# A convolution and gated low-rank experts in split float32: first two tiles multiplied whole, low parts of the weights made later, kernel block spread from SBUF, table arguments on ScalarE

## The chip, the cores and the metric

One program runs on one core of a Trainium2 chip. The metric is the device time of one execution in microseconds; lower is better. The engines are TensorE (PE, its weight loads are PEld), VectorE (DVE), ScalarE (ACT), GpSimd (POOL) and SyncE (SP), which issues most of the DMAs. Each takes its instructions in the order in which they are written, and they wait for each other by semaphores.

## What is computed

```python
H, L = 64, 1024                      # heads, length; the batch is 64
dtA = (-exp(log_A_real) + 1j * A_imag) * exp(log_dt)[:, None]
K = 2 * einsum('hn,hnl->hl', Cs, exp(dtA[:, :, None] * arange(L))).real
y = causal_convolution(u * mask, K) + u * mask * D      # by FFT here
y = y * mask
scores = y @ Wr.T                                        # 64 experts
gates = softmax(top_k(scores, 16)), 0 elsewhere
h = einsum('nd,krd->nkr', y, A)                          # rank 16 each
out = x + 2.0 * einsum('nkr,kdr->nd', h * gates, B)
```

`x` is (64, 64, 1024) in float32, so 4096 rows of 1024 pass through the product with `A` (1024 x 1024), the router (1024 x 64) and the product with `B` (1024 x 1024).

## The kernel before, in words

The work is cut into 32 tiles (`TILES`) of two heads (`HT`) by 64 batches, which is 128 rows each. Every matrix product is made of three products in the format float32r: each operand is split into a high part (`*_hi`, a copy made by ScalarE) and a low part (`*_lo`, the subtraction `arrived - hi` made by VectorE), and hi x hi, hi x lo and lo x hi are summed in PSUM. The weights `a` and `b` are loaded once and stay in SBUF, in 17 pieces (`loads`: the router, eight of `A`, eight of `B`).

For a tile there are five kinds of work.

- **Tables.** `arguments(t)` on VectorE computes `args = grid * turns + phases`, for two heads and two phases of 130 elements, and takes the whole turns off. `waves(t)` on ScalarE makes `turned` (a sine) and `decay` (two exponentials); each of the two functions needs another table in ScalarE, so there is an `ACT_TABLE_LOAD` ahead of each. `make_powers(t)` multiplies the two, and `out_factors(t)` gives `out_raw`.
- **Convolution.** It runs in chunks of 128 positions. `turn_in` and `feed` on TensorE give what each chunk adds to a state, `first_states` and `states` on VectorE carry the state through seven chunks, `kernel_row` gives 128 values of `K`. ScalarE copies them to `k_sb` (`copy_k`), `add_skip` adds `D`, and two DMAs (`kernel_rows`, then `load_near`) take them to a padded row in HBM and back as a 128 x 128 block `t_lo`, in which each row stands one to the side of the row above. `near` multiplies with that block, `from_states` with the states.
- **Up.** `mask_y` masks the result, and `product_high` and `product_low` multiply it with `A` and the router in three column ranges (`H_PARTS`, 320 + 384 + 384 columns).
- **Gates.** `scores` go through two rounds of `max` and `match_replace` and two exponentials to `gates`; `hg` is the product of `h` and the gates, in three instructions, one per range.
- **Down.** `turn_hg` transposes `hg` in two halves, ScalarE copies them to `g_hi`, and 48 products of 512 columns with `B` give `out_ps`; `x_in` gets the rows of `x` plus the scaled result and is written out.

The work is staggered by hand. While `step(t)` multiplies tile t, it makes the states of tile t+1, the convolution's factors of tile t+2 and the tables of tile t+3. The order within each engine is that of the code. On TensorE a step is: the up products, `turn_hg` of half of `hg`, `near(t+1)`, `turn_hg` of the rest, `from_states(t+1)`, `turn_in(t+2)`, three quarters of the down products, `kernel_row(t+2)`, the rest of them, `feed(t+2)`. On VectorE, step t+1 follows directly on these rows of step t:

```python
dve.scalar_tensor_tensor(out=x_in[:, columns], ...)   # half 0
add_skip(t + 2)
make_powers(t + 3)       # waits for decay from ScalarE
dve.scalar_tensor_tensor(out=x_in[:, columns], ...)   # half 1
first_states(t + 2); states(t + 2, range(1, MIDDLE))  # now step t+1
# scores, top 16
states(t + 2, range(MIDDLE, FED))
# gates, hg in three parts
```

Ahead of step 0 stands a long start: the constants of the tables, and the low parts of all 17 pieces of the weights. `FIRST_B` products need the pieces of `A`, the down products those of `B`.

## Time and profile before

| | us |
|---|---|
| median of three runs | 970.09 (969.84 to 970.32) |
| the profiled execution's own time | 970.01 |
| its span, first to last instruction | 968.2 |
| PE busy | 909.8 (94%) |
| DVE busy | 734.9 (76%) |
| ACT busy | 350.6 (36%) |

The median is the time of the whole execution, and the span is what the profile's clock covers; 1.8 us lie around the span. The mean granted clock of TensorE over the span is 0.988 of full speed. A busy share is an average over a start, a long repeated part and an end, which have different limits.

### The profile page before, as it was taken

The numbers are of one execution on the slowest core, as the hardware profiler recorded it, in microseconds if no ns is written. First come the engines' busy times: TensorE is split into PE (matmuls) and PEld (weight loads), VectorE is DVE, ScalarE is ACT, GpSimd is POOL, SyncE is SP. The second block draws the span as 40 slices with busy tenths as digits, with TensorE's granted clock in tenths as the row PEclk, the third lists the DMA queues.
The fourth block names the chain that finished last, engine by engine and source line by source line (L and its number), as shares of the span: only waits on it lengthen the run. The fifth ranks groups of instructions, "written<-read, shape, count | busy, mean of one in ns | idle before, by whom it ended". The sixth has DMA issues, their size and how long they took to land.

```text
span 968.2 us, 15861 instructions
## 1 busy us (share of the span) xinstructions
PE 909.8 (94%) x4800; PEld 821.6 (85%) x4800; DVE 734.9 (76%) x2520; ACT 350.6 (36%) x569; POOL 1.3 (0%) x10
## 2 busy tenths in 40 slices
PE   0376999999999999999999999999999999999998
PEld 0265999988899998889999888999998899999887
DVE  7887877777788777778877777887777788777642
ACT  5543342334424333342333334333333433423210
POOL 0000000000000000000000000000000000000000
PEclk9977999999999999999999999999999999999999
DMA  7310212211221222112122211222221122222101
GB/s 272 145 50 22 67 54 70 70 52 51 59 70 49 70 70 62 49 54 67 49 70 70 70 49 49 65 53 66 70 70 49 49 65 64 55 70 71 48 25 44
DMA packets 27676, 63.63 MB, mean 66 GB/s; under 512 B 4816, under 2 KB 13200, under 8 KB 27664
## 3 DMA queue, kind: packets, MB, share of 16 engines
q1 hardware_dynamic: 27664, 63.49, 22.6%
q8 instruction: 6, 0.10, 0.0%
q14 instruction: 6, 0.05, 0.0%
HBM read 46.63 MB, written 16.84 MB: 66 GB/s over the span
## 4 chain that ended last, share of the span: by engine, by line
PE 91%; DVE 6%; ACT 1%; issue 1%; SPq 0%; DMA 0%; DVEq 0%; ACTq 0%
PE out_ps L751 24%; PE h_ps L751 18%; PE out_ps L755 12%; PE h_ps L755 9%; PE turn_ps L751 8%; PE turn_ps L755 4%; PE turn_ps L760 3%; PE conv_ps L736 2%; PE conv_ps L735 2%; PE conv_ps L734 2%; PE conv_ps L745 1%; PE conv_ps L746 1%; PE conv_ps L744 1%; PE conv_ps L727 1%; PE conv_ps L726 1%; PE conv_ps L725 1%
## 5 line engine op out<-in xcount | busy, mean ns | idle before, releaser
L751 PE MATMUL out_ps<-b_hi,g_hi 128*128 128x512 f32 x512 | 203.6, 398 | 0.0
L751 PE MATMUL out_ps<-b_lo,g_hi 128*128 128x512 f32 x512 | 200.5, 392 | 0.0
L751 PE MATMUL h_ps<-a_hi,y_hi 128*128 128x384 f32 x512 | 172.1, 336 | 0.0
L751 PE MATMUL h_ps<-a_lo,y_hi 128*128 128x384 f32 x512 | 172.0, 336 | 0.0
L755 PE MATMUL out_ps<-b_hi,g_lo 128*128 128x512 f32 x512 | 129.3, 395 | 0.0
L755 PEld LDWEIGHTS out_ps<-b_hi,g_lo 128*128 128x128 f32 x512 | 96.1, 188 | 22.4
L751 PEld LDWEIGHTS out_ps<-b_hi,g_hi 128*128 128x128 f32 x512 | 96.3, 188 | 19.3
L751 PEld LDWEIGHTS out_ps<-b_lo,g_hi 128*128 128x128 f32 x512 | 96.2, 188 | 19.2
L425 DVE TENSOR_TENSOR powers<-turned,decay 128x520 f32<-128x520 f32 x32 | 22.4, 700 | 110.6 <-ACT decay L283 110.5
L482 DVE SCALAR_TENSOR_TENSOR z<-swapped,step_other,part 128x64 f32<-128x64 f32 x384 | 92.4, 282 | 11.0
L755 PE MATMUL h_ps<-a_hi,y_lo 128*128 128x384 f32 x512 | 99.2, 336 | 0.0
L475 DVE SCALAR_TENSOR_TENSOR part<-z,step_own,conv_ps 128x64 f32<-128x64 f32 x384 | 90.5, 277 | 8.9
L751 PEld LDWEIGHTS h_ps<-a_hi,y_hi 128*128 128x128 f32 x512 | 96.1, 188 | 0.0
L751 PEld LDWEIGHTS h_ps<-a_lo,y_hi 128*128 128x128 f32 x512 | 96.1, 188 | 0.0
L688 DVE SCALAR_TENSOR_TENSOR x_in<-out_ps,gate_scale,x_in 128x512 f32<-128x512 f32 x64 | 47.9, 748 | 60.7 <-PE out_ps L755 60.7
L755 PEld LDWEIGHTS h_ps<-a_hi,y_lo 128*128 128x128 f32 x512 | 89.7, 188 | 0.0
L359 ACT ACTIVATE exp_all<-score_sb,neg_max 128x64 f32<-128x64 f32 x32 | 11.1, 348 | 206.7 <-DVE neg_max L634 206.7
L751 PE MATMUL turn_ps<-a_hi,y_hi 128*128 128x320 f32 x256 | 77.1, 314 | 2.0 <-DVE a_lo L503 2.0
L751 PE MATMUL turn_ps<-a_lo,y_hi 128*128 128x320 f32 x256 | 77.0, 314 | 0.0
L367 ACT ACTIVATE g_hi<-turn_ps 128x512 fp32r<-128x512 f32 x64 | 38.4, 600 | 83.7 <-PE turn_ps L760 83.7
L299 ACT ACTIVATE k_sb<-h_ps 1x256 f32<-1x256 f32 x32 | 12.0, 375 | 149.2 <-PE h_ps L716 149.0
L307 ACT ACTIVATE z_hi<-z 128x896 fp32r<-128x896 f32 x32 | 30.5, 954 | 95.0 <-DVE z L482 95.0
(159 smaller groups left out, 1479.8 us busy)
## 6 DMA issues: line engine op xcount, KB each, us to landing
xt_in<-in_xt SPq DMA_DIRECT2D x32, 512.0 KB, 3.3
x_in<-in_x SPq DMA_DIRECT2D x64, 256.0 KB, 3.6
out<-x_in SPq DMA_DIRECT2D x62, 256.0 KB, 3.1
a_in<-in_a_t SPq DMA_DIRECT2D x8, 512.0 KB, 8.9
b_in<-in_b_t SPq DMA_DIRECT2D x8, 512.0 KB, 14.4
t_lo<-k_padded SPq DMA_DIRECT2D x32, 128.0 KB, 2.9
k_padded<-k_sb SPq DMA_DIRECT2D x32, 1.0 KB
out<-x_in SPq DMA_DIRECT2D x4, 128.0 KB, 2.3
```

The lines of the kernel that those rows point to most:

```text
L307: act.activation(z_hi[:, :, :, :], z[:, :, :, :], ACT.Copy).then_inc(s_zhi, 1)
L367: act.activation(g_hi[:, 4 * bank:4 * bank + 4, :].rearrange("p c n -> p (c n)"), turn_ps[:, bank, :], ACT.Copy).then_inc(s_ghi, 1)
L425: dve.tensor_tensor(out=powers[:, :, :, :], in0=turned[:, :, :, :], in1=decay[:, :, :].unsqueeze(2).to_broadcast([P, HT, 2, W]), op=ALU.mu ...
L475: dve.scalar_tensor_tensor(out=part[:, i, :], in0=z[:, c - 1, i, :], scalar=step_own[:, bass.ds(n + i, 1)], in1=conv_ps[i][:, c * B:(c + 1 ...
L482: dve.scalar_tensor_tensor(out=z[:, c, i, :], in0=swapped[:, i, :], scalar=step_other[:, bass.ds(n + i, 1)], in1=part[:, i, :], op0=ALU.mu ...
L688: dve.scalar_tensor_tensor(out=x_in[:, columns], in0=out_ps[:, half, :], scalar=gate_scale[:, :], in1=x_in[:, columns], op0=ALU.mult, op1= ...
L734: pe.matmul(conv_ps[i][:, :], t_hi[:, i, :], xt_hi[:, i, :], start=True, stop=False)
L735: pe.matmul(conv_ps[i][:, :], t_hi[:, i, :], xt_lo[:, i, :], start=False, stop=False)
L736: last = pe.matmul(conv_ps[i][:, :], t_lo[:, i, :], xt_hi[:, i, :], start=False, stop=False)
L751: pe.matmul(o, hi[:, c, :], moving[:, c, columns], start=first and c == order[0] and moving is w_hi, stop=False)
L755: last = pe.matmul(o, lo[:, c, :], w_hi[:, c, columns], start=False, stop=c == order[-1])
L760: last = pe.transpose(turn_ps[:, c // 4, (c % 4) * P:(c % 4 + 1) * P], hg[:, c * P:(c + 1) * P], ident[:, :])
```

## The change

It has four parts.

1. **Whole float32 for tiles 0 and 1** (`EXACT = 2`). The products of these two tiles (feed, kernel row, near, from states, up) multiply float32 operands as they are (`whole_*`), and the splits of `out_raw`, `xt`, `z`, `y`, `in` and `t` are dropped for them. The down products keep the three float32r products. The first tile's convolution gets its output in `out_ps` in two halves (`conv_0`), so that the first half of `y` can be masked and multiplied early.
2. **Low parts later.** Four pieces of `B` (`EARLY`) get their low parts from TensorE and ScalarE: `whole_b` computes `arrived - hi` in PSUM with an identity and a negated identity, ScalarE copies it out. Four (`MIDST`) stay on VectorE ahead of step 0. The nine pieces of `A` and the router (`LATE`) are subtracted by VectorE in step 1. The remaining loads are issued behind `load_near(0)`.
3. **The block from SBUF.** `k_sb` is now itself padded, and `load_near` reads the shifted rows straight out of its one partition, in one DMA per head. The write to HBM is gone.
4. **Arguments on ScalarE.** From tile 1 on the four rows `grid * turns + phase` are four ScalarE instructions (`theta`), each with a scale and a bias that are read from a column. `waves(t)` becomes `sines(t)`, `theta(t + 1)`, `decays(t)`. Half of the parameter loads are issued by ScalarE.

The diff, cut to what matters:

```diff
+EXACT = 2
...
+        EARLY = [FIRST_B + c for c in (4, 5, 6, 7)]
+        MIDST = [FIRST_B + c for c in (3, 2, 1, 0)]
+        LATE = list(range(FIRST_B))
+        HIGH = EARLY + LATE[:3] + MIDST + LATE[3:]
+        REST_PS = [turn_ps, out_ps, turn_ps, out_ps]
...
             def load_near(t, first=False):
                 if not first:
                     sp.wait_ge(s_near, t)
-                    sp.sem_inc(s_freed, 1)
-                sp.wait_ge(s_k, 16 * t + 16)
-                src = bass.AP(k_dram, t * (HT * KROW), [[1, P], [KROW, HT], [1, P]])
-                sp.dma_start(t_lo[:, :, :].bitcast(F32), src).then_inc(s_t, 16)
+                sp.wait_ge(s_kdone, t + 1)
+                for i in range(HT):
+                    row = k_sb[:, i, :]
+                    shifted = bass.AP(row.tensor, row.offset, [[HT * KROW, 1], [1, P], [1, P]])
+                    sp.dma_start(t_lo[:, i, :].bitcast(F32), shifted).then_inc(s_t, 16)
...
-            def waves(t):
-                act.wait_ge(s_args, t + 1)
-                act.activation(turned[:, :, :, :], args[:, :, :, :], ACT.Sin, scale=TWO_PI).then_inc(s_wave, 1)
-                for i in range(HT):
-                    act.activation(decay[:, i, :], grid[:, 0, :], ACT.Exp, scale=rates[:, bass.ds(HT * t + i, 1)]).then_inc(s_wave, 1)
+            def theta(t):
+                act.wait_ge(s_sine, t)
+                for i in range(HT):
+                    turn = turns[:, bass.ds(HT * t + i, 1)]
+                    act.activation(args[:, i, 0, :], grid[:, :], ACT.Identity, scale=turn, bias=phase_own[:, :]).then_inc(s_theta, 1)
+                    act.activation(args[:, i, 1, :], grid[:, :], ACT.Identity, scale=turn, bias=phase_other[:, :]).then_inc(s_theta, 1)
...
                 if table:
-                    waves(t + 3)
+                    sines(t + 3)
+                    if not last_table:
+                        theta(t + 4)
+                    decays(t + 3)
             step(0, first=True)
-            with act.Fori(LOOP, END) as t:
+            step(1)
+            with act.Fori(LOOP, END - 1) as t:
                 step(t)
+            step(TILES - 4, last_table=True)
...
             def arguments(t):
-                for i in range(HT):
-                    dve.scalar_tensor_tensor(out=args[:, i], in0=grid[:, :, :], scalar=turns[:, bass.ds(HT * t + i, 1)],
-                                             in1=phases[:, :, :], op0=ALU.mult, op1=ALU.add).then_inc(s_theta, 1)
-                dve.wait_ge(s_theta, HT * t + HT)
+                dve.wait_ge(s_theta, 2 * HT * t + 2 * HT)
...
+            step(1, weights=LATE)
...
+            def whole_b(n):
+                _, arrived, hi, _ = loads[EARLY[n]]
...
+                for half in range(2):
+                    columns = slice(half * HALF, (half + 1) * HALF)
+                    pe.matmul(REST_PS[n][:, half, :], ident[:, :], arrived[:, columns], start=True, stop=False)
+                    last = pe.matmul(REST_PS[n][:, half, :], minus[:, :], hi[:, columns], start=False, stop=True)
...
+            def whole_product(n, c):
+                o, c0, width, _ = H_PARTS[n]
+                return pe.matmul(o, y_m[:, c, :], a_in[:, c, c0:c0 + width], start=c == 0, stop=c == NC - 1)
...
+            pe.wait_ge(s_minus, 3)
+            whole_b(0)
             turn_in(0)
-            feed(0, first=True)
-            kernel_row(0)
-            near(0)
-            from_states(0)
...
+            whole_b(1)
+            whole_feed(0)
+            whole_row(0, k_ps)
+            whole_b(2)
+            whole_b(3)
+            whole_near_0()
+            whole_from_states_0(0)
+            first_step()
+            step(1, whole=True)
+            pe.wait_ge(s_wlo, len(MIDST) + len(LATE))
```

Three places in the order of the instructions carry the prediction. The first is the end of ScalarE's repeated step, from the copy of the kernel row (`k_sb`) to the end of the loop. Before:

```order
L299 ACTIVATE k_sb<-h_ps 1x256
L280 REGISTER_ALU
L281 ACT_TABLE_LOAD
L281 ACTIVATE turned<-args 128x520
L283 ISA
L283 ACT_TABLE_LOAD
L283 ACTIVATE decay<-grid,rates 128x130
L283 ISA
L283 ACTIVATE decay<-grid,rates 128x130
```

The same place in the changed kernel:

```order
L335 ACTIVATE k_sb<-h_ps 1x2x128
L307 REGISTER_ALU
L308 ACT_TABLE_LOAD
L308 ACTIVATE turned<-args 128x520
L303 ISA
L303 ACTIVATE args<-grid,phase_own,turns 128x130
L304 ACTIVATE args<-grid,phase_other,turns 128x130
L303 ISA
L303 ACTIVATE args<-grid,phase_own,turns 128x130
L304 ACTIVATE args<-grid,phase_other,turns 128x130
L314 ISA
L314 ACT_TABLE_LOAD
```

Four instructions now stand between the sine and the table load that the two `decay` rows follow.

The second place is VectorE's step 1 of the changed kernel, from the low part of the gated `hg` (`g_lo`) to the add of the first half of `x_in`:

```order
L730 TENSOR_TENSOR g_lo<-turn_ps,g_hi 128x512 x2
L551 TENSOR_TENSOR y_m<-conv_ps,mask 128x8x64 x2
L497 TENSOR_TENSOR o_lo<-out_raw,o_hi 128x260
L501 TENSOR_TENSOR in_lo<-h_ps,in_hi 128x256
L571 TENSOR_TENSOR a_lo<-a_in,a_hi 128x8x64
L571 TENSOR_TENSOR a_lo<-a_in,a_hi 128x1024 x3
L565 TENSOR_TENSOR y_lo<-y_m,y_hi 128x8x64 x2
L515 TENSOR_TENSOR xt_lo<-xt_in,xt_hi 128x1024
L571 TENSOR_TENSOR a_lo<-a_in,a_hi 128x1024 x5
L470 TENSOR_SCALAR turned<-args 128x520
L472 TENSOR_TENSOR args<-args,turned 128x520
```

Nine subtractions for the weights stand there that stood ahead of step 0 before, and the two rows of `arguments` are behind them.

The third place is the start of TensorE, up to the first product with `A`. Before, the first rows were two transposes, the feed, the kernel row and the near products in threes:

```order
L709 MATMUL h_ps<-ident,powers 128x128 x2
L725 MATMUL conv_ps<-xt_hi,in_hi 128x448
L726 MATMUL conv_ps<-xt_lo,in_hi 128x448
L727 MATMUL conv_ps<-xt_hi,in_lo 128x448
L725 MATMUL conv_ps<-xt_hi,in_hi 128x448
```

In the changed kernel the subtractions for `b` stand around them:

```order
L845 MATMUL h_ps<-ident,powers 128x128 x2
L837 MATMUL out_ps<-b_in,ident 128x512
L838 MATMUL out_ps<-b_hi,minus 128x512
L837 MATMUL out_ps<-b_in,ident 128x512
L838 MATMUL out_ps<-b_hi,minus 128x512
L874 MATMUL conv_ps<-xt_in,in_whole 128x448 x2
L856 MATMUL h_ps<-out_raw,real 128x256
```

Each threefold product has become a single one on whole operands, and four products for a piece of `b` come ahead of the feed; two more pieces follow before the near products.

## Rows read from the trace of the kernel before

**Rows 1.** The page: the span.
```profile
span 968.2 us, 15861 instructions
```

**Rows 2.** Busy time by stretch: us, PE, PEld, DVE, ACT, POOL (instructions), PE clock, DMA.
```profile
50.00:60.00 10.00, 7.52 (x25) 6.79 (x26) 7.28 (x11) 3.28 (x6) 0.00 (x0) 0.50 0.37 106
70.00:80.00 10.00, 0.00 (x0) 0.00 (x0) 9.17 (x35) 1.72 (x4) 0.00 (x0) 0.71 0.00 0
491.00:519.00 28.00, 28.00 (x151) 25.37 (x150) 21.89 (x76) 10.23 (x18) 0.00 (x0) 1.00 0.22 61
```

**Rows 3.** Timeline of PE: start, duration, what, idle before; tiles 0, 0, 1, 16.
```profile
55.06 0.60 PE L751 MATMUL turn_ps<-a_hi,y_hi 128*128 128x320 f32 x1 [2.01 <-DVE a_lo L503]
...
80.36 1.11 PE L760 MATMUL turn_ps<-ident,hg 128*128 128x128 f32 x4 [10.77 <-DVE hg L658]
...
98.60 0.31 PE L751 MATMUL turn_ps<-a_hi,y_hi 128*128 128x320 f32 x1
...
519.90 0.31 PE L751 MATMUL turn_ps<-a_hi,y_hi 128*128 128x320 f32 x1
```

**Rows 4.** Busy groups of VectorE until 98.6 us: busy us, mean ns, idle before.
```profile
L503 DVE TENSOR_TENSOR b_lo<-b_in,b_hi 128x1024 fp32r<-128x1024 f32 x8 | 9.3, 1219 | 0.2 <-ACT b_hi L276 0.2
L503 DVE TENSOR_TENSOR a_lo<-a_in,a_hi 128x1024 fp32r<-128x1024 f32 x8 | 9.2, 1218 | 0.0
```

**Rows 5.** Waits between 300 and 600 us: total us, times, longest us.
```profile
DVE powers L425 <- ACT decay L283: 37.2, 10, 3.7
...
DVE x_in L688 <- PE out_ps L755: 14.3, 11, 1.3
```

**Rows 6.** Timeline from a kernel row on TensorE to the powers on VectorE.
```profile
514.86 0.28 PE L716 MATMUL h_ps<-o_lo,real 128*128 128x256 f32 x1
...
515.18 0.38 ACT L299 ACTIVATE k_sb<-h_ps 1x256 f32<-1x256 f32 x1 [4.91 <-PE h_ps L716]
...
517.52 1.28 ACT L283 ACT_TABLE_LOAD   x1
...
518.82 0.70 ACT L283 ACTIVATE decay<-grid,rates 128x130 f32<-128x130 f32 x2
519.55 0.70 DVE L425 TENSOR_TENSOR powers<-turned,decay 128x520 f32<-128x520 f32 x1 [3.72 <-ACT decay L283]
```

**Rows 7.** Timeline of `hg` on VectorE and the weight loads that need it.
```profile
502.65 0.55 DVE L658 TENSOR_TENSOR hg<-h_ps,gates 128x384 f32<-128x384 f32 x1
504.51 0.55 DVE L658 TENSOR_TENSOR hg<-h_ps,gates 128x384 f32<-128x384 f32 x1
...
503.49 0.53 PEld L760 LDWEIGHTS turn_ps<-ident,hg 128*128 128x128 f32 x4
...
505.26 0.59 PEld L760 LDWEIGHTS turn_ps<-ident,hg 128*128 128x128 f32 x4
```

**Rows 8.** Busy groups of ScalarE over the span.
```profile
L283 ACT ACTIVATE decay<-grid,rates 128x130 f32<-128x130 f32 x64 | 22.4, 397 | 0.4
...
L359 ACT ACTIVATE exp_all<-score_sb,neg_max 128x64 f32<-128x64 f32 x32 | 11.1, 348 | 206.7 <-DVE neg_max L634 206.7
...
L276 ACT ACTIVATE b_hi<-b_in 128x1024 fp32r<-128x1024 f32 x8 | 7.7, 1043 | 0.0
...
L333 ACT ACTIVATE far_decay<-rates 128x64 f32<-128x64 f32 x1 | 0.3, 256 | 0.0
```

**Rows 9.** Timeline: parameter loads on the SP queue, first powers on VectorE.
```profile
0.74 3.63 SPq L211 DMA_DIRECT2D par<-in_parameters  x8
...
18.39 0.70 DVE L425 TENSOR_TENSOR powers<-turned,decay 128x520 f32<-128x520 f32 x1
```

**Rows 10.** The chain that ended last, at full clock: start, us, what.
```profile
102.29 2.78 PE h_ps L751 x16
...
110.61 0.44 PE turn_ps L760 x4
```

**Rows 11.** DMA issues: count, KB each, median us from issue to landing.
```profile
t_lo<-k_padded SPq DMA_DIRECT2D x32, 128.0 KB, 2.9
```

More of the change, by code:

```diff
@@ L250, in step @@
                     fetch_rows(t + 1)
-            step(0)
+            for t in range(LOOP):
+                step(t)
             with sp.Fori(LOOP, END) as t:
@@ L368, in step @@
                                    ACT.Copy).then_inc(s_ghi, 1)
+                if first:
+                    for i in LATE[6:]:
+                        split_weights(i)
+                    sines(2)
+                    theta(3)
+                    decays(2)
                 if prep:
@@ L371, in step @@
                     high_in(t + 2)
-                if conv:
+                if conv and not first:
                     for i in range(HT):
@@ L396, in link, with mark, after @@
                 dve.wait_ge(s_calc, calc[0])
+            def mark(ins):
+                calc[0] += 1
+                ins.then_inc(s_calc, 1)
+                return calc[0]
+            def after(count):
+                dve.wait_ge(s_calc, count)
             def exp_parts(v):
@@ new lines, in _ @@
+            dve.tensor_tensor(out=u, in0=a, in1=a, op=ALU.mult)
+            squares = mark(dve.tensor_tensor(out=v, in0=aim, in1=aim, op=ALU.mult))
+            after(angle)
+            nearest = mark(dve.tensor_scalar(kk, im, INV_2PI, ROUND, ALU.mult, ALU.add))
+            after(squares)
+            square = mark(dve.tensor_tensor(out=den, in0=u, in1=v, op=ALU.add))
+            after(nearest)
+            nearest = mark(dve.tensor_scalar(kk, kk, ROUND, None, ALU.subtract))
+            dve.tensor_copy(skip[:, :], par[0:1, 5, :])
@@ new lines, in add_rows, with first_step @@
+            def add_rows(t, half):
+                columns = slice(half * HALF, (half + 1) * HALF)
+                dve.wait_ge(s_down, 2 * t + half + 1)
+                dve.scalar_tensor_tensor(out=x_in[:, columns], in0=out_ps[:, half, :], scalar=gate_scale[:, :],
+                                         in1=x_in[:, columns], op0=ALU.mult, op1=ALU.add).then_inc(s_o, 1)
+            def first_step():
+                gate(0)
+                gates_of(0)
+                gate_part(0, 0)
+                gate_part(0, 1)
+                sum_gates()
+                first_states(1)
+                add_skip(1)
+                states(1, range(1, 3))
+                gate_part(0, 2)
+                states(1, range(3, 5))
+                low_gated(0, 0)
+                low_gated(0, 1)
+                states(1, range(5, FED))
+                arguments(2)
+                make_powers(2)
+                out_factors(2)
+                for i in range(HT):
+                    mask_y(1, i)
+                low_in(2)
+                low_out(2)
+                low_x(2)
+                scale_of(0)
+                add_rows(0, 0)
+                arguments(3)
+                add_skip(2)
+                make_powers(3)
+                add_rows(0, 1)
@@ new lines, in step @@
+            def step(t, conv=True, prep=True, table=True, weights=()):
+                if conv:
+                    first_states(t + 1)
+                    states(t + 1, range(1, MIDDLE))
+                gate(t)
+                if conv:
+                    states(t + 1, range(MIDDLE, FED))
+                gates_of(t)
+                gate_part(t, 0)
+                gate_part(t, 1)
+                if conv:
+                    low_near(t + 1)
+                    low_z(t + 1)
+                sum_gates()
+                gate_part(t, 2)
@@ L673, in step @@
                     low_in(t + 2)
+                for i in weights[:4]:
+                    low_weights(i)
                 if conv:
@@ L773, in step, with turn_hg, down_high @@
                     if n == 0:
-                        pe.wait_ge(s_ylo, HT * t + HT)
+                        pe.wait_ge(s_ylo, HT * (t - EXACT) + HT)
                     product_low(o, y_lo, a_hi, slice(c0, c0 + width), range(NC)).then_inc(s_up, 1)
+            def turn_hg(blocks):
+                for c in blocks:
+                    last = pe.transpose(turn_ps[:, c // 4, (c % 4) * P:(c % 4 + 1) * P], hg[:, c * P:(c + 1) * P], ident[:, :])
+                return last
+            def down_high(half, order, first=False):
+                product_high(out_ps[:, half, :], g_hi, b_hi, b_lo, slice(half * HALF, (half + 1) * HALF), order, first)
@@ new lines, in step @@
+            def step(t, conv=True, prep=True, whole=False):
+                pe.wait_ge(s_glo, 2 * t)
+                if whole:
+                    pe.wait_ge(s_ym, HT * t + HT)
+                    pe.wait_ge(s_kcopy, t + 2)
+                    for n in range(len(H_PARTS)):
+                        for c in range(NC):
+                            last = whole_product(n, c)
+                        last.then_inc(s_up, 1)
+                else:
+                    pe.wait_ge(s_yhi, HT * (t - EXACT) + HT)
+                    up(t, conv)
```

527 lines of the change are left out of this document (302 added, 225 removed).

## The prediction

> **What bounds the kernel now.** I read the page first (the span [rows 1]), then the busy time by stretch. In a stretch of 28 us in the middle TensorE is busy for all of it and VectorE for 21.9 [rows 2]: the repeated part is bound by TensorE. A tile takes (519.90 - 98.60) / 15 = 28.09 us [rows 3]. The start is another matter: tile 1 begins only at 98.60, after a gap of 10.77 us in which TensorE waits for `hg`, because VectorE has 9.2 + 9.3 us of subtractions for the weights in its queue [rows 3, 4]. So the start can be shortened, and the rest can only get longer, by a wait of TensorE.
>
> The next question is how near such a wait is, since the change adds work to ScalarE in every tile. The waits of the middle say that VectorE stands idle 3.7 us per tile ahead of `powers`, for `decay` [rows 5]. Such an idle time looks like slack, and it is none. The timeline shows a loop. TensorE makes a kernel row at 514.86, ScalarE copies it at 515.18, and only then come the sine, the table load and `decay`; VectorE makes `powers` at 519.55 [rows 6]. Behind it stand the second half of `x_in`, the states of the next tile, the gates and `hg`. One period before, at 519.55 - 28.09 = 491.46, the same `powers` began, and the second part of `hg` ended at 502.65 + 0.55 = 503.20, 11.74 us later [rows 6, 7]. Of VectorE's idle time per tile (28.0 - 21.9 = 6.1 [rows 2]) 3.7 lie ahead of `powers` and 1.3 ahead of `x_in` [rows 5], so this stretch is nearly without a gap. TensorE loads that part of `hg` at 503.49; the third part ends at 504.51 + 0.55 = 505.06 and is loaded at 505.26 [rows 7]. With 0.04 us for the signal (`decay` ends at 519.52, `powers` begins at 519.55 [rows 6]) the slack is 0.25 and 0.16 us. Whatever makes `decay` later by more than 0.16 us makes TensorE wait in every tile.
>
> **The repeated part after the change.** `theta` puts four ScalarE rows between the sine and the table load ahead of `decay`. VectorE loses its two rows of `arguments` in return, but these are ahead of the wait for `down` (1.3 us idle [rows 5]) and gain nothing there. The price of a row: `decay` has 130 elements and one operand read from a column and takes 0.397; two of them take 0.70, so one overlaps the next by 0.10 [rows 6, 8]. `theta` has a second such operand, its bias. `exp_all` (64 elements, a bias column) takes 0.348 and `far_decay` (64, none) 0.256 [rows 8], so I add 0.09: 0.49 each. Four take 4 x 0.49 - 3 x 0.10 = 1.66, and 0.04 for the wait for the sine makes 1.70. The wait of TensorE is 1.70 - 0.16 = 1.54 us per tile. The lower bound is a second column that costs nothing: 4 x 0.397 - 0.3 + 0.04 = 1.33, a wait of 1.17. The upper is no overlap: 1.96 + 0.04, a wait of 1.84. I take the middle one, since each part of it has a row. Which tiles: a `theta` row in step t delays `hg` of tile t+1. It stands in the steps to 27, so tiles 3 to 28 wait, 26 of them (tiles 1 and 2 are counted in the start): 26 x 1.54 = 40.0 us, with 30.4 and 47.8 as bounds.
>
> **The start after the change**, by when each piece begins.
> - First powers: 18.39 before. Eight parameter loads take 3.63 us of issuing on one queue [rows 9]; split over two queues they take half, and land 1.4 us earlier after the first of the others. About 2 us of small operations move behind `powers`. I take 15.0.
> - Price of products: 16 of 384 columns take 2.78, so a column costs 0.45 ns at full clock [rows 10]. A whole float32 product holds all four products of two halves by two halves, and the split form three of them, so I count four times the float32r time. The nearest row is lower: four transposes of float32 operands take 0.44 for 4 x 128 columns, 0.86 ns, 1.9 times [rows 10]; that is my lower bound.
> - The Trainium skill says in FP8 and Floating Point Precision, under TensorE Precision Notes, that true FP32 needs four passes through the array. By that the sum stays; by the transposes' row it would be 3 us less. No row here shows such a product.
> - Clock: the stretch from 50 to 60 us runs at 0.50, the lower level of 1.2 GHz, after TensorE had mostly idled [rows 2]. I count the low level until about 23 us.
> - Transposes 15.8 to 16.5, the copy and a 1.04 us copy of a piece of `b` [rows 8] to 18.2; `whole_b(1)` is 2 x 512 x (4 + 1) columns, 4.6 at the low clock, to 22.8; the feed 896 x 4 columns, 3.2, to 26.0; the row and two more pieces of `b` 0.5 + 4.6 + waits to 31.4; a copy, near products and the first half of the states' 1.2 + 2.6 to 35.2; mask. First up product at 36.2, against 55.06 [rows 3]: it no longer waits for the low parts of `a`.
> - Up products of tile 0: 8 x 1088 columns x 4 x 0.45 ns = 15.8; a transpose, a feed, a row and a half of the states lie in between, 3.2; a last wait of 1.1 for `hg`. `turn_hg` at 56.3, against 80.36 [rows 3].
> - From there to tile 1 it took 98.60 - 80.36 = 18.2 and takes about the same (two fewer high-low triples, two whole products). Tile 1 begins at 74.4, 24.2 earlier.
> - Tile 1: its up products take 15.8 where 24 x 1088 columns took 11.8, + 4.0. The kernel row of tile 2 now follows the whole of the down products, and `theta` comes into the loop, a wait of 1.3. And VectorE has nine subtractions, 9.2 + 0.6 us [rows 4], in this step, all ahead of `arguments`; tile 2 waits for them, 1.6. Together + 6.9.
> - Tile 2: `arguments`, sine and `decay` stand behind these subtractions, so `powers` comes about 5.5 us after the tile's first product instead of 0.35 before it (519.55 against 519.90 [rows 3, 6]). Less the slack that is 5.7 us of waiting.
> - Tile 3 began at 98.60 + 2 x 28.09 = 154.8 and now begins 24.2 - 6.9 - 5.7 = 11.6 us earlier.
>
> The block from SBUF replaces two DMAs in a row by one. In the repeated part nobody waits for it: it is issued at about 516 [rows 6] and used after 503.49 + 28.09 = 531.6 [rows 7], with 2.9 us to landing [rows 11]. In the start I count the same 2.9. The Trainium skill says in SBUF — State Buffer, under Door 1: The DMA port swizzle, that a DMA's bandwidth goes by the number of 16 ports its partitions reach; one partition reaches one. An estimate from its 435 GB/s over 16 ports is 27 GB/s, 4.8 us for the 128 KB. It would delay the near products of tile 0 by some 2 us and end at 1000; no row here has a DMA out of one partition.
>
> **Sum.** 968.2 - 11.6 + 40.0 = 996.6 us of span, + 1.8 around it (970.01 - 968.2) = 998.4. The profiled execution is 0.08 below the median, which is nothing here. I say 998.
>
> **Rivals.**
> - *The delay is absorbed* (faster). If ScalarE runs the four rows in little time, or VectorE's stretch behind `powers` has slack that I don't see, the start's gain remains, and grows, since tiles 1 and 2 wait 1.3 and 1.6 us less: 11.6 + 2.9 = 14.5, so 955.5. It decides where 26 waits equal the gain: about 0.5 us per tile, that is four rows in 0.7. For it speaks that the idle time ahead of `powers` is long; against it every row above: two `decay` rows alone take 0.70 [rows 8, 6]. 8 in 100.
> - *The clock falls in each wait.* TensorE ran at the low level at 55.06, behind a gap of 2.0 us [rows 2, 3]. If 1.5 us of waiting brought 5 us at half speed in each tile, as from 55.06 to 60, it would cost 2.5 us more in each of 26: 1063. Against it: before 55 us it had been idle most of the time, and would be busy 95% here. 4 in 100.
> - *The start gains nothing*: the clock stays low to 40 us and beyond, or the late loads of `a` and `b` hold up the up products. Then 970.0 + 40.0 + about 4 = 1014. 6 in 100.
> - The forecast has 81 in 100, and 1 is left for a sum that ends within 0.2%.
>
> **Numbers.** The start gives 11.6, with 19 if the float32 products cost 1.9 times and the clock is full from the first, and 4 if it is low until 40 us and the block is late. The low end is 970.0 + 30.4 - 19 = 981, the high end 970.0 + 47.8 - 4 = 1014; I take 980 to 1014. A change of 0.2% (1.9 us) is about what a measurement of this kernel can tell from none. Faster: 8 in 100; the same: 1; slower: 91.
>
> **What would show it.** In the middle, TensorE waits about 1.5 us per tile ahead of `turn_hg`, released by `hg`, the period is 29.6 us, and `powers` waits 5.4 for `decay`. Four ScalarE rows of 0.49 stand between sine and table load. Tile 1 begins near 74, tile 2 near 109, tile 3 near 143, with a wait of 5 to 6 us in tile 2. Wrong would be a period of 28.1, `theta` rows under 0.2 us, or a tile 3 at 155.

## The result and the profile after

The changed kernel takes 998.75 us, the median of 4 runs (997.6 to 1001.69), the kernel before 970.02. The ratio is 1.0299, 95% interval [1.0287, 1.0311]: slower by 3%. The forecast was 998.0. The profiled execution of the changed kernel took 997.6 us, the fastest of the four; its span is the row below.

**The page of the changed kernel**: the span.

```profile
span 995.8 us, 15699 instructions
```

**Timeline of TensorE, changed kernel**: the first up product of tile 0, the first transpose of tile 0's `hg`, tile 1, tile 1's `hg`, tile 2, tile 2's `hg`, tile 3 and tile 16. These answer to [rows 3].

```profile
35.21 0.78 PE L937 MATMUL turn_ps<-a_in,y_m 128*128 128x320 f32 x2 [0.96 <-issue]
...
54.21 0.98 PE L950 MATMUL turn_ps<-ident,hg 128*128 128x128 f32 x7 [1.11 <-DVE hg L723]
...
72.27 4.47 PE L937 MATMUL turn_ps<-a_in,y_m 128*128 128x320 f32 x16
76.57 10.48 PE L937 MATMUL h_ps<-a_in,y_m 128*128 128x384 f32 x32
89.34 0.66 PE L950 MATMUL turn_ps<-ident,hg 128*128 128x128 f32 x4 [2.28 <-DVE hg L723]
...
107.49 0.41 PE L928 MATMUL turn_ps<-a_hi,y_hi 128*128 128x320 f32 x1 [1.72 <-DVE a_lo L571]
...
124.48 1.11 PE L950 MATMUL turn_ps<-ident,hg 128*128 128x128 f32 x4 [4.87 <-DVE hg L723]
...
142.89 0.31 PE L928 MATMUL turn_ps<-a_hi,y_hi 128*128 128x320 f32 x1
...
527.73 0.31 PE L928 MATMUL turn_ps<-a_hi,y_hi 128*128 128x320 f32 x1
```

The start is shorter by 154.8 - 142.89 = 11.9 us at tile 3. From there a tile takes (527.73 - 142.89) / 13 = 29.60 us, where it took 28.09. The waits of the middle say why (between 300 and 600 us: total us, times, longest us), beside [rows 5]:

```profile
DVE powers L479 <- ACT decay L314: 54.2, 10, 5.4
...
PEld turn_ps L950 <- DVE hg L723: 17.4, 20, 1.5
PE turn_ps L950 <- DVE hg L723: 11.9, 10, 1.2
```

VectorE now waits 5.4 us for `decay` instead of 3.7, and TensorE, which waited for nothing here, stops in every tile for `hg`: its weight loads 1.5 us, its transposes 1.2 us, since the loads had run ahead of the products. The loop itself, in the changed kernel's timelines of ScalarE, VectorE and the weight loads (against [rows 6, 7]):

```profile
495.22 0.64 ACT L308 ACTIVATE turned<-args 128x520 f32<-128x520 f32 x1
496.00 0.50 ACT L303 ACTIVATE args<-grid,phase_own,turns 128x130 f32<-128x130 f32 x1
496.40 0.48 ACT L304 ACTIVATE args<-grid,phase_other,turns 128x130 f32<-128x130 f32 x1
496.79 0.48 ACT L303 ACTIVATE args<-grid,phase_own,turns 128x130 f32<-128x130 f32 x1
497.18 0.48 ACT L304 ACTIVATE args<-grid,phase_other,turns 128x130 f32<-128x130 f32 x1
497.68 1.28 ACT L314 ACT_TABLE_LOAD   x1
498.97 0.70 ACT L314 ACTIVATE decay<-grid,rates 128x130 f32<-128x130 f32 x2
...
499.70 0.70 DVE L479 TENSOR_TENSOR powers<-turned,decay 128x520 f32<-128x520 f32 x1 [5.42 <-ACT decay L314]
...
510.88 0.55 DVE L723 TENSOR_TENSOR hg<-h_ps,gates 128x384 f32<-128x384 f32 x1
...
511.48 0.42 PEld L950 LDWEIGHTS turn_ps<-ident,hg 128*128 128x128 f32 x4 [1.51 <-DVE hg L723]
```

Read it as a chain: the sine ends at 495.86, the table load that `decay` needs starts at 497.68. The four rows between, with 0.14 us of waiting for the sine ahead of them, take 1.82 us. `powers` follows 0.03 us behind `decay`, the second part of `hg` ends 11.73 us after `powers` began (511.43; before it was 11.74), and its load follows at 511.48, 1.51 us late. Nothing on the way has absorbed the delay.

Busy time of the changed kernel by stretch (us; PE, PEld, DVE, ACT, POOL; PE clock; DMA), beside [rows 2]:

```profile
124.00:130.00 6.00, 5.52 (x19) 4.74 (x20) 4.16 (x11) 1.53 (x3) 0.00 (x0) 0.57 0.00 0
491.00:519.00 28.00, 26.82 (x145) 24.16 (x144) 19.42 (x73) 11.97 (x21) 0.00 (x0) 1.00 0.31 61
```

In the middle the clock stays at its full level, 2.4 GHz, in spite of a wait in every tile. Behind the 4.87 us wait of tile 2 it does not: 0.57 over 6 us.

### The profile page after: what moved, and what is told of

It reads as the page before. It is cut to its first block, busy times and chain, and to the rows that moved or that the text cites. A ratio compares the mean times of both kernels' runs of the same rounds, so it can differ in the third digit from the quotient of the medians.

```text
span 995.8 us, 15699 instructions
## 1 busy us (share of the span) xinstructions
PE 933.1 (94%) x4772; PEld 817.2 (82%) x4772; DVE 693.2 (70%) x2443; ACT 392.7 (39%) x685; POOL 2.0 (0%) x12
## 4 chain that ended last, share of the span: by engine, by line
PE 43%; DVE 28%; ACT 15%; issue 10%; DMA 1%; DVEq 1%; ACTq 1%; SPq 0%
PE out_ps L928 18%; DVE z L542 7%; PE out_ps L932 6%; DVE swapped L537 5%; DVE part L535 5%; ACT L314 4%; ACT L308 3%; PE turn_ps L950 3%; DVE x_in L743 2%; ACT decay L314 2%; DVE hg L723 2%; ACT turned L308 2%; ACT args L303 2%; PE h_ps L928 2%; ACT args L304 2%
## 5 line engine op out<-in xcount | busy, mean ns | idle before, releaser
L928 PE MATMUL h_ps<-a_hi,y_hi 128*128 128x384 f32 x480 | 163.3, 340 | 0.0
L928 PE MATMUL h_ps<-a_lo,y_hi 128*128 128x384 f32 x480 | 161.6, 337 | 0.0
L932 PEld LDWEIGHTS out_ps<-b_hi,g_lo 128*128 128x128 f32 x512 | 96.1, 188 | 21.2
L932 PE MATMUL h_ps<-a_hi,y_lo 128*128 128x384 f32 x480 | 94.5, 339 | 0.0
L928 PEld LDWEIGHTS h_ps<-a_lo,y_hi 128*128 128x128 f32 x480 | 90.2, 188 | 0.0
L928 PEld LDWEIGHTS h_ps<-a_hi,y_hi 128*128 128x128 f32 x480 | 90.0, 188 | 0.0
L932 PEld LDWEIGHTS h_ps<-a_hi,y_lo 128*128 128x128 f32 x480 | 85.3, 188 | 0.0
L950 PE MATMUL turn_ps<-ident,hg 128*128 128x128 f32 x256 | 41.1, 285 | 39.4 <-DVE hg L723 39.4
L950 PEld LDWEIGHTS turn_ps<-ident,hg 128*128 128x128 f32 x256 | 28.0, 143 | 56.4 <-DVE hg L723 55.7
L928 PE MATMUL turn_ps<-a_hi,y_hi 128*128 128x320 f32 x240 | 71.0, 309 | 1.7 <-DVE a_lo L571 1.7
L928 PE MATMUL turn_ps<-a_lo,y_hi 128*128 128x320 f32 x240 | 70.8, 309 | 0.0
```

The costliest lines, as they stand in the source:

```text
L928: pe.matmul(o, hi[:, c, :], moving[:, c, columns], start=first and c == order[0] and moving is w_hi, stop=False)
L932: last = pe.matmul(o, lo[:, c, :], w_hi[:, c, columns], start=False, stop=c == order[-1])
L950: last = pe.transpose(turn_ps[:, c // 4, (c % 4) * P:(c % 4 + 1) * P], hg[:, c * P:(c + 1) * P], ident[:, :])
```

## The experiments

The period of a kernel is read in its trace from two starts of the transposes of `powers` in the repeated part, 26 tiles apart. For the changed kernel:

```profile
130.21 0.38 PE L845 MATMUL h_ps<-ident,powers 128*128 128x128 f32 x2
...
899.96 0.38 PE L845 MATMUL h_ps<-ident,powers 128*128 128x128 f32 x2
```

(899.96 - 130.21) / 26 = 29.61 us. All kernels read in this way, with the median of the runs and the interval of the ratio to the kernel before:

| kernel | time, us | ratio to before | period, us |
|---|---|---|---|
| before | 970.0 | 1 | 28.09 |
| changed | 998.75 | 1.0287 to 1.0311 | 29.61 |
| decay_first | 956.24 | 0.9839 to 0.9871 | 28.16 |
| half_theta | 976.07 | 1.0046 to 1.008 | 28.83 |
| theta_alone | 1014.75 | 1.0438 to 1.0473 | 29.64 |
| args_vector | 964.17 | 0.992 to 0.9953 | 28.36 |
| spare_tile | 965.88 | 0.9941 to 0.9974 | 28.36 |
| rows_hbm | 959.71 | 0.9885 to 0.992 | 28.16 |
| args_early | 954.2 | 0.9818 to 0.9851 | 28.16 |
| decay_ahead | 955.6 | 0.9839 to 0.9871 | 28.16 |
| shift_32 | 960.31 | 0.9887 to 0.9923 | 28.36 |
| shift_1072 | 957.64 | 0.9861 to 0.9894 | 28.27 |
| before_32 | 968.22 | 0.9972 to 0.9991 | 28.03 |
| theta_twice | 1064.78 | 1.0929 to 1.1053 | 32.20 |

The first theory was that the argument rows stand in the loop's chain, ahead of `decay`, and that this alone loses what the start gains. The rival was that the whole products, the block from SBUF or a slower clock make the repeated part slower.

### decay_first: the same work, two calls exchanged

```diff
                 if table:
                     sines(t + 3)
+                    decays(t + 3)
                     if not last_table:
                         theta(t + 4)
-                    decays(t + 3)
```

> Changed kernel with one pair swapped in every step: the two decay rows ahead of the four theta rows. ScalarE does the same work, VectorE too. Loop theory (a delay of decay by 1.70 us turns into 1.5 us of waiting of TensorE in each of tiles 3 to 28): the waits for hg are gone in the middle, the period is 28.1 us again, and the time is about 998.75 - 26 x 1.51 - 3 (tiles 1 and 2) = 956 us. Rival (the sum of ScalarE's work, or the block read from SBUF, is what made it slower): nothing changes, 998 us.

Measured: 956.24 us. ScalarE does all the work of the change, and no wait of TensorE is listed in the middle. The timeline of ScalarE in `decay_first`:

```profile
502.60 0.64 ACT L308 ACTIVATE turned<-args 128x520 f32<-128x520 f32 x1
503.26 1.28 ACT L314 ACT_TABLE_LOAD   x1
504.55 0.70 ACT L314 ACTIVATE decay<-grid,rates 128x130 f32<-128x130 f32 x2
```

The table load follows the end of the sine by 0.02 us, not by 1.82, and the period is 28.16 us. So the 42.5 us between this kernel and the changed one are the place of four rows. Between the two profiled spans it is 995.8 - 954.8 = 41.0 us: 26 x 1.45 = 37.7 in tiles 3 to 28, and 3.5 ahead of tile 3, which begins at 139.43 here and at 142.89 in the changed kernel. This settles the theory for the repeated part. It also prices the rest of the change: 970.0 - 956.2 = 13.8 us are gained. Tile 3 begins 154.78 - 139.43 = 15.4 us earlier than in the kernel before, and each period is 0.07 us longer.

### half_theta: two rows ahead of decay, two behind

```diff
                     if not last_table:
-                        theta(t + 4)
+                        theta(t + 4, range(0, 1))
                     decays(t + 3)
+                    if not last_table:
+                        theta(t + 4, range(1, HT))
```

> Changed kernel with two of the four theta rows ahead of decay and two behind it. Loop theory: decay comes later by 0.5 + 0.4 + 0.1 = 0.9 instead of 1.7 us, so the wait per tile is 0.8 less, about 0.75: 998.75 - 26 x 0.78 - 1.5 = 977 us. If the wait were not proportional (a threshold, a clock that falls in each wait), it would be near 956 or near 998.

Measured: 976.07 us, a period of 28.83. Two rows cost 28.83 - 28.16 = 0.67 us per tile, four cost 29.61 - 28.16 = 1.45. How much later `decay` comes with two rows is read from ScalarE's timeline of this kernel:

```profile
484.32 0.64 ACT L308 ACTIVATE turned<-args 128x520 f32<-128x520 f32 x1
...
486.00 1.28 ACT L314 ACT_TABLE_LOAD   x1
```

The sine ends at 484.96, the table load follows 1.04 us behind it. Four rows put `decay` 1.82 - 0.02 = 1.80 us later and lengthen the period by 1.45: 0.35 us are absorbed. Two rows put it 1.04 - 0.02 = 1.02 us later and lengthen the period by 0.67: again 0.35. Two delays give one slack, and beyond it the delay goes into the period one for one.

### theta_alone: the kernel before with this part of the change only

```diff
+            def theta(t):
+                ...
-            def waves(t):
+            def waves(t, next_theta=False):
                 ...
                 act.activation(turned[:, :, :, :], args[:, :, :, :], ACT.Sin, scale=TWO_PI).then_inc(s_wave, 1)
+                if next_theta:
+                    theta(t + 1)
                 for i in range(HT):
                     act.activation(decay[:, i, :], ...)
...
             def arguments(t):
-                for i in range(HT):
-                    dve.scalar_tensor_tensor(out=args[:, i], ...)
+                if isinstance(t, int) and t < 4:
+                    for i in range(HT):
+                        dve.scalar_tensor_tensor(out=args[:, i], ...)
```

> Kernel before with part 4 alone: four theta rows on ScalarE between sine and decay from tile 4 on, VectorE's two rows gone. Loop theory: each of tiles 1 to 28 waits 1.5 us for hg: 970 + 28 x 1.52 = 1012.6 us, period 29.6. Rival (the cost needs the other parts beside it): 970 us.

Measured: 1014.75 us. The waits of its middle (between 300 and 600 us):

```profile
DVE powers L437 <- ACT decay L293: 55.1, 10, 5.5
...
PEld turn_ps L772 <- DVE hg L670: 15.9, 20, 1.4
```

They are close to those of the changed kernel (5.4 and 1.5), without whole products, later low parts or a block from SBUF. The wait needs none of these. The period is 29.64 - 28.09 = 1.55 us longer. The forecast was 1012.6; 1.3 of the 2.1 us above it lie ahead of tile 1, which begins at 99.88 and not at 98.60, and the rest is the period.

### args_vector: the argument rows back on VectorE from tile 5

```diff
             def arguments(t):
+                if not (isinstance(t, int) and t <= 4):
+                    for i in range(HT):
+                        dve.scalar_tensor_tensor(out=args[:, i], ...)
```

ScalarE makes the four rows no more from tile 5 on.

> Changed kernel with arguments back on VectorE from tile 5 on (part 4 undone in the repeated part). Loop theory: 956 us, as with decay ahead, since VectorE has 0.9 us of room ahead of its wait for the down products; period 28.1. Rival (the other parts of the change cost something in the repeated part): a period above 28.1 and a time between 960 and 998.

Measured: 964.17 us, 8 more than expected. No wait of TensorE is listed in the middle, but the period is 28.36 and not 28.16, 5.6 us over 28 tiles; the other 2 are in the start (tile 3 begins at 141.36, in `decay_first` at 139.43). A period that is longer without a wait means instructions that take longer. This kernel keeps a table of phases of 1040 bytes a partition, which moves the tiles behind it. The next four experiments are about that.

### spare_tile: decay_first with a tile that nothing reads

```diff
         grid = sb("grid", [P, W])
+        spare = sb("spare", [P, 2, W])
...
+            pool.memset(spare[:, :, :], 0.0)
```

> decay_first with one more tile of 128x260 float32 that nothing reads (zeroed once by GpSimd), placed where the kernel with the arguments on VectorE keeps its table of phases; b_hi, z_hi, z_lo, xt_hi and xt_lo lie 1 KB higher and nothing else changes. The period of a tile was 28.16 us in decay_first and 28.36 us in args_vector, without a wait of TensorE in either. If the addresses of the tiles set the pace of the products: period 28.36, 956.2 + 28 x 0.20 = 962 us. If it is the arguments on VectorE that cost the 0.20: period 28.16, 956 us.

Measured: a period of 28.36, exactly that of `args_vector`. So the 0.20 us per tile have nothing to do with VectorE's rows: they come from where the tiles lie. The profiled execution took 961.8 us, as expected, the three others 965.8 to 966.2. The mean granted clock is 0.992 in each of the three and 0.995 in the profiled one, so some 3 of the 4 us are time at the lower level (0.003 of 964 us, an estimate); why they had more of it is open.

### shift_32, shift_1072 and before_32: which address

```diff
+        spare = sb("spare", [P, 8])
         b_hi = sb("b_hi", [P, NE, D], F32R)
```

The first two add their tile to `args_early` (below), `before_32` to the kernel before, ahead of its `scratch` tiles; in `shift_1072` it is `[P, 268]`.

> args_early with a tile of 32 bytes a partition, zeroed once and read by nothing, ahead of b_hi: b_hi, z_hi, z_lo, xt_hi and xt_lo lie 32 bytes higher, b_hi at byte 179072 of a partition instead of 179040. If the pace of the products hangs on whether these tiles begin at a multiple of 64 bytes (as b_hi does in spare_tile and args_vector, with periods of 28.36 us, and does not where the period is 28.16): period 28.36 and 954.2 + 28 x 0.20 = 960 us. If it hangs on the distance of about 1 KB that spare_tile added: period 28.16 and 954 us.

> args_early with such a tile of 1072 bytes, so that the same five tiles lie 1072 bytes higher (b_hi at 180128, half way between multiples of 64, and 32 bytes above its place in spare_tile). If the remainder by 64 decides: period 28.16 and 954 us. If the distance decides: period 28.36 and 960 us.

> The kernel before with a tile of 32 bytes ahead of its first-used tiles, so that of the tiles of the repeated part b_hi alone moves, from 194880 (a multiple of 64) to 194912. If the remainder decides and the kernel before pays for it too: the period falls from 28.09 us by up to 0.2, and 970.0 becomes 965 to 968 us. If the place of b_hi is not what matters, or the change's own tiles brought it: period 28.09, 970 us.

Measured: 28.36, 28.27 and 28.03 us. The groups of the third down product between 400 and 700 us (busy us, mean ns), in the order before, `before_32`, `args_early`, `shift_32`, `shift_1072`, a fence for each:

```profile
L755 PE MATMUL out_ps<-b_hi,g_lo 128*128 128x512 f32 x176 | 44.5, 394 | 0.0
```
```profile
L757 PE MATMUL out_ps<-b_hi,g_lo 128*128 128x512 f32 x176 | 43.8, 391 | 0.0
```
```profile
L934 PE MATMUL out_ps<-b_hi,g_lo 128*128 128x512 f32 x176 | 43.8, 391 | 0.0
```
```profile
L936 PE MATMUL out_ps<-b_hi,g_lo 128*128 128x512 f32 x168 | 42.6, 395 | 0.0
```
```profile
L936 PE MATMUL out_ps<-b_hi,g_lo 128*128 128x512 f32 x169 | 42.3, 392 | 0.0
```

Where `b_hi` begins at a multiple of 64 bytes (before, `shift_32`) this product takes 394 to 395 ns, where it begins 32 bytes beside one 391 to 392. In `before_32`, where of the tiles of the repeated part `b_hi` alone moves, and by 32 bytes, that is worth 1.8 us (ratio 0.9972 to 0.9991). That the address counts is shown. That the remainder by 64 is the rule is not: `shift_1072` has the good one for all five tiles (they lie 1088 bytes higher, 180128 against 179040) and ends between the two, at 28.27. In it the third down product is back at 392 ns, but the first (`b_hi` with `g_hi`) stays at 401 ns, as in `shift_32`, against 397 in `args_early`, and `z_hi` with `o_hi` at 412, again as in `shift_32`, against 404.

### rows_hbm: the kernel rows through HBM again

```diff
-                sp.wait_ge(s_kdone, t + 1)
-                for i in range(HT):
-                    row = k_sb[:, i, :]
-                    ...
+                sp.wait_ge(s_k, 16 * t + 16)
+                for i in range(HT):
+                    shifted = bass.AP(k_dram, (HT * t + i) * KROW, [[1, P], [1, P]])
```

> decay_first with part 3 undone: the kernel rows go to HBM as a padded row and the block is read from there, in two loads. Theory: the way through SBUF is not slower in total, since one load of 6.3 us replaces a write and a load that took 4.6 + 2.9 us in the kernel before; only the first block is waited for (3.2 us), so tile 0's states come 1 to 2 us later here and the time is 957 to 958 us, the period 28.16. Rival: the load out of one partition is the slower way (5.4 us to landing against 2.9) and its 3.2 us wait goes away: 953 us.

Measured: 959.71 us, 3.5 above `decay_first`, and the same period. In `decay_first` the block is asked for at 23.50 and first used at 30.39 (issue on SP's queue, then TensorE):

```profile
23.50 1.18 SPq L219 DMA_DIRECT2D t_lo<-k_sb  x2
...
30.39 3.68 PE L901 MATMUL out_ps<-xt_in,t_lo 128*128 128x256 f32 x8 [3.25 <-DMA t_lo<-k_sb]
```

In `rows_hbm` two transfers follow each other, with weight loads issued between them:

```profile
22.98 0.32 SPq L216 DMA_DIRECT2D k_padded<-k_sb  x1
...
25.15 0.98 SPq L224 DMA_DIRECT2D t_lo<-k_padded  x2
...
33.35 2.93 PE L909 MATMUL out_ps<-xt_in,t_lo 128*128 128x256 f32 x6 [6.73 <-DMA t_lo<-k_padded]
```

6.9 us from the first issue to the first product against 10.4: the difference is the whole 3.5 us. It is not the price of HBM alone. Four weight loads of 512 KB are issued between the write and the read here, and behind the block in `decay_first`; how the way through HBM would do without them ahead of it was not tried. In the repeated part a half of the block lands 2.7 us after its issue from HBM and 5.4 us from SBUF, and the period is the same: there the place costs nothing either way.

### args_early and decay_ahead: a shorter start

```diff
+                if table and weights:
+                    arguments(t + 3)
                 for i in weights[4:]:
                     low_weights(i)
-                if table:
+                if table and not weights:
                     arguments(t + 3)
```

> decay_first, and in the second step the subtraction of the whole turns for tile 4 stands ahead of VectorE's five last low parts of a instead of behind them. Theory: powers of tile 4 then don't wait for ScalarE (1.9 us less), the low parts come 1.1 us later, and of the 3.0 us wait for the gated activations of tile 2 about 1.9 goes, with part of the slow clock behind it: 956.2 - 1.9 - 0.5 = 953.8 us, between 952.5 and 955. Rival: what the low parts lose is all that is gained, since VectorE is busy throughout: 956 to 957 us.

Measured: 954.2 us. Powers of tile 4 on VectorE, in `decay_first` and then in `args_early`:

```profile
109.81 0.70 DVE L479 TENSOR_TENSOR powers<-turned,decay 128x520 f32<-128x520 f32 x1 [1.87 <-ACT decay L314]
```
```profile
108.67 0.68 DVE L479 TENSOR_TENSOR powers<-turned,decay 128x520 f32<-128x520 f32 x1
```

The wait of 1.87 us is gone; the low parts of `a` come later by their share, so that TensorE waits 2.84 us for them instead of 1.77, and at most 1.1 us for `hg` instead of 2.99. The net is 2.0 us. Behind these 2.84 us the clock fell too (0.72 over 108 to 114 us). This is the fastest kernel here: it beats the one before by 1.5 to 1.8% and the changed one by 44.5 us.

```diff
+                if table:
+                    decays(t + 3)
                 if prep:
                     high_x(t + 2)
                     copy_k(t + 2)
                 if table:
                     sines(t + 3)
-                    decays(t + 3)
                     if not last_table:
                         theta(t + 4)
```

> args_early, and ScalarE makes the decays before it copies the kernel row, in its idle time and while its exponential's table is still loaded; the four argument rows stand behind the sine as in the changed kernel, but nothing on the chain waits for them. Theory: the loop through the states has 2 us more slack, the period stays 28.16 us (TensorE bounds it), and the waits of tiles 1 and 2 for gated activations shrink by up to 1.9 us more: 952 us, between 950 and 954. Rival: VectorE's own work bounds tiles 1 and 2 and this changes nothing against args_early; or the decays delay the copy of the kernel row and the high parts for TensorE, and the period grows.

Measured: 955.6 us (954.26 to 956.88), against 953.69 to 954.95 for `args_early`; `decays(2)` also stands earlier in the first step. The period is 28.16: with TensorE as the bound more slack on ScalarE buys nothing (VectorE now waits 1.7 us ahead of `powers` instead of 3.6). The first rival was right: nothing is gained against `args_early`. The waits of tiles 1 and 2 for `hg` are gone, and in their place TensorE stands still for 2.0 us ahead of the `feed` of tile 2 (at 72.47) and for 2.7 us for the low parts of `a`.

### theta_twice: twice the wait

```diff
                 act.wait_ge(s_sine, t)
+                if not isinstance(t, int):
+                    for i in range(HT):
+                        turn = turns[:, bass.ds(HT * t + i, 1)]
+                        act.activation(again[:, i, 0, :], ...)
+                        act.activation(again[:, i, 1, :], ...)
```

> The changed kernel, and in each of the 26 steps of its loop ScalarE makes its four argument rows twice, first into a tile that nothing reads. Four more rows at 0.39 us from start to start make decay 1.57 us later, and TensorE waits 3.0 us in every tile instead of 1.4. Theory: the wait grows one for one and the clock stays at its full level: period 29.60 + 1.57 = 31.17 us, 998.75 + 26 x 1.57 = 1039.6 us. Rival: a wait of 3 us brings the slow clock behind it, as after the waits of 4.9 us and 3.0 us in tile 2 of the changed kernel and of decay_first; then 1.5 to 3 us more are lost in each tile: 1080 to 1120 us, with a mean granted clock well under 0.99.

Measured: 1064.78 us, 25 above the theory and 15 below the rival. Both are half right. In the trace 11 of the 26 periods are 31.14 to 31.17 us, just the expected 31.17. The other 15 are 32.4 to 33.9, and all together they lose 27.0 us (837.17 - 26 x 31.16). A tile of the first kind and one of the second, in the timeline of TensorE:

```profile
415.52 0.66 PE L956 MATMUL turn_ps<-ident,hg 128*128 128x128 f32 x4 [2.72 <-DVE hg L729]
...
446.68 0.65 PE L956 MATMUL turn_ps<-ident,hg 128*128 128x128 f32 x4 [2.73 <-DVE hg L729]
...
447.65 0.39 PE L889 MATMUL conv_ps<-xt_hi,t_lo 128*128 128x512 f32 x1
447.88 0.59 PE L887 MATMUL conv_ps<-xt_hi,t_hi 128*128 128x512 f32 x1
448.27 0.63 PE L888 MATMUL conv_ps<-xt_lo,t_hi 128*128 128x512 f32 x1
```

and the clock behind them, by stretch:

```profile
415.00:419.00 4.00, 3.48 (x20) 3.01 (x21) 4.00 (x11) 1.58 (x3) 0.00 (x0) 1.00 0.00 0
448.00:452.00 4.00, 4.00 (x17) 3.38 (x15) 3.19 (x9) 0.60 (x1) 0.00 (x0) 0.58 0.00 0
```

Products of 512 columns follow each other at 0.23 us until 447.88 and at 0.43 us behind it: the clock goes from 2.4 to 1.2 GHz while TensorE is busy again, over a microsecond after the wait's end. After equal waits of 2.7 us it falls in some tiles and not in others, and in a fixed order: three tiles of 31.15 us (two at the first time), then four of 32.7, 33.9, 32.4 and 32.7, and so on through the loop. What decides that was not tried. The length of the wait alone does not: tile 1 of `args_vector` and tile 1 of the changed kernel have equal waits at 88.6 and 89.3 us (2.29 and 2.28), and the clock over 89 to 94 us is not the same, first `args_vector`, then the changed kernel:

```profile
89.00:94.00 5.00, 5.00 (x22) 4.21 (x21) 3.80 (x10) 1.22 (x3) 0.00 (x0) 0.66 0.00 2
```
```profile
89.00:94.00 5.00, 4.66 (x26) 3.96 (x27) 5.00 (x13) 2.19 (x6) 0.00 (x0) 1.00 0.01 2
```

## Why the prediction was right

- **The loop has almost no slack.** Right, and the size was off by half: the slack was read as 0.16 us, `half_theta` and the changed kernel both give 0.35. The prediction measured it up to the weight load (505.26, 0.20 us behind the end of the third part of `hg`). But the load ran 0.23 us ahead of its product there. The transposes of that part, in the kernel before and then the part and its transposes in the changed kernel:

```profile
505.49 0.60 PE L760 MATMUL turn_ps<-ident,hg 128*128 128x128 f32 x4
```
```profile
512.74 0.55 DVE L723 TENSOR_TENSOR hg<-h_ps,gates 128x384 f32<-128x384 f32 x1
...
513.39 0.61 PE L950 MATMUL turn_ps<-ident,hg 128*128 128x128 f32 x4
```

  They start 505.49 - 505.06 = 0.43 us behind the part, and 513.39 - 513.29 = 0.10 where they wait for it. The slack up to the product is 0.33 us by these rows.
- **Price of the four rows.** 0.49 us each was forecast, 0.48 to 0.50 was measured, and the overlap of 0.10 too. The wait for the sine costs 0.14 us (495.86 to 496.00) and not 0.04, so `decay` is later by 1.80, not 1.70. The errors of delay (+0.10) and slack (+0.19) nearly cancel: that the wait came out as 1.45 against 1.54 is in part luck.
- **26 waits.** 26 x (29.61 - 28.09) = 39.5 us against 40.0. Of the 1.52 only 1.45 are the wait: the period of the changed kernel is 28.16 without it (`decay_first`).
- **That 0.07** was no term of the sum. In the before kernel an up product of 384 columns takes 336 ns, in the changed one 337 to 340 (the page's groups); in the trace of `decay_first` every fourth one is followed by the next after 180 ns and not 174. From start to start these products take 8.48 us per tile there and 8.32 before, 0.16 more, and the down products 11.10 against 11.16. `theta_alone`, without whole products, and `args_vector`, with the argument rows on VectorE, have the slower up products as well, so neither the whole products nor the rows on ScalarE make them. What does is open. In the sum the 0.07 made up for most of the 0.09 by which the wait was forecast too long.
- **The start.** Tile 3 was forecast at 143.2 and began at 142.89. The pieces were off by more: the first powers came at 14.02 instead of 15.0, the up products at 35.21 instead of 36.2, `hg` of tile 0 at 54.21 instead of 56.3, tile 1 at 72.27 instead of 74.4. The clock reached its full level at about 17 us (two transposes took 0.63 us at 15.38 and take 0.38 at 130.21; the first row below follows), where I had counted the low one until 23. From the first powers to the first up product it took 21.2 us all the same, as forecast, and that is luck: the block took the gain back, since TensorE waited 3.2 us for it, and behind this wait the clock fell again (the second row).

```profile
20.00:25.00 5.00, 4.72 (x15) 2.38 (x13) 3.53 (x19) 3.17 (x6) 0.00 (x0) 1.00 0.09 4
...
30.00:34.00 4.00, 4.00 (x12) 3.29 (x12) 0.00 (x0) 0.20 (x1) 0.00 (x0) 0.57 1.02 417
```

- **Whole float32 products.** I counted four times the split's. In the rows above 8 products of 320 columns take 76.57 - 72.27 = 4.30 us (the profile shows two records for each), 0.54 each; as float32r they start 0.147 apart (24 of them from 142.89 to 146.41). That is 3.7 times, and the lower bound of 1.9 is out. By the Trainium skill (FP8 and Floating Point Precision, TensorE Precision Notes) it would be four passes; the trace nearly agrees.
- **The block from SBUF.** I counted 2.9 us to landing, and this term was wrong. In the start it took 6.9 us from the first issue (23.03) to the first product (29.92), TensorE waiting. In the repeated part the median is 5.4 us to landing for each half of the block, and nobody waits, as forecast. The Trainium skill's rule (SBUF — State Buffer, Door 1: The DMA port swizzle), by which a DMA's bandwidth goes by the ports that its partitions reach, gave an estimate of 4.8 us for both halves; that is nearer than 2.9, and still too short.
- **Tiles 1 and 2.** Tile 1 took 107.49 - 72.27 = 35.22 us, 7.1 more than 28.09, where 6.9 were forecast. In tile 2 a wait of 5.7 us was forecast and 4.87 came. What I had missed is behind it: the products from 124.5 to 129.2 ran at 1.2 GHz. Tile 2 took 142.89 - 107.49 = 35.40 us, 7.3 more than 28.09, against the 5.7.
- **Luck in the start.** Tile 1 began 2.1 us earlier than forecast, and tiles 1 and 2 lost 0.2 and 1.6 us more. So the 11.9 us at tile 3 against 11.6 are errors that cancel, not a start that was understood to 0.3 us.
- **Rivals.** *Absorbed* would have given 955.5; `decay_first` shows that this is the time once the rows leave the chain (956.24), so the rival's price was right and its condition was not met. *The clock falls in each wait* was wrong for waits of 1.5 us and half right for waits of 2.7. The row that it came from did not bear on it: the low level of 55.06 was there ahead of the gap of 2.0 us (in the kernel before, products of 448 columns start 0.37 us apart at 51 us, and 0.20 at full clock). *The start gains nothing* was wrong by 12 us.

## What to carry to other kernels

Idle time of an engine is slack only if nothing comes round to it again: follow the loop from the idle engine back to itself over one period, and take the smallest gap on the way as the slack, on TensorE up to the product and not to its weight load. New work on a half-idle engine belongs behind the last instruction of that loop, not ahead of it; here the exchange of two calls was worth 42.5 us. When a period changes while no wait does, compare mean durations of the same instruction: the tiles may only have moved. Errors that cancel in a sum show only where each piece is compared with its row.

## What the hardware showed that was not expected

- The product of `b_hi` with `g_lo` took 394 to 395 ns where `b_hi` begins at a multiple of 64 bytes, and 391 to 392 where it begins 32 bytes beside one. The other products did not all follow this (`shift_1072`). An unread tile of 32 bytes made the kernel before 1.8 us faster and `args_early` 6.1 us slower (960.31 - 954.2).
- The clock fell behind waits of 4.87 (changed kernel), 2.99 (`decay_first`) and 2.84 us (`args_early`) and behind 15 of 26 waits of 2.7 us (`theta_twice`). Of two waits of 2.3 us it fell behind one (`args_vector`, tile 1) and not behind the other (changed kernel, tile 1). It never fell in the middle of the changed kernel, where the waits are 1.2 to 1.5 us.
- It can fall late: 1.2 us after TensorE had started again (447.88 against 446.68).
- A load of a 128 by 128 block out of one partition, 64 KB, took 5.4 us to landing, where one from HBM took 2.7 (`rows_hbm`) and both halves from HBM in one transfer 2.9 [rows 11]. The way through HBM needs a write first: in the start, with four weight loads between, it took 3.5 us longer in all.
